# A state-space layer whose row split moves to GpSimd, whose load block is merged, and whose result is added to x by TensorE

## The reference, cut to what matters

```python
xn = layernorm(layernorm(x)) * gamma + beta
u, z = split(xn @ in_w.T)              # 256 features each
u = silu(causal_conv(u, 4 taps) + conv_b)
x_dbl = u @ xproj_w.T                  # 8 dt ranks, 16 B rows, 16 C rows
dt = softplus(x_dbl[:8] @ dt_w.T + dt_b)
for t in time:                         # 16 states for each feature
    h = exp(dt * A) * h + dt * B * u
    y = sum_n(h * C)
y = (y + u * D) * silu(z)
out = y @ out_w.T
# result: x + layernorm(x) + out_fwd + out_bwd
```

## Time and profile before

| | us |
|---|---|
| median of three runs | 2711.14 (2708.47 to 2712.14) |
| the profiled execution | 2711.35 |
| its span, first to last instruction | 2709.6 |
| first `step` of the layer | 69.28 |
| last x added in the layer | 1030.76 |
| VectorE busy in the span | 2064.6 (76%) |
| TensorE busy in the span | 2362.9 (87%) |
| GpSimd busy in the span | 1190.6 (44%) |

### The profile page before, as it was taken

The page is one execution under the profiler, slowest core; times in us unless marked ns, Lnnn a source line. Parts: engine busy times, 40 slices in busy tenths (PEclk is TensorE's granted clock), DMA queues, the critical chain, the costliest instruction groups (busy, mean ns, idle before and its releaser), DMA issues. The chain is left out here.

```text
span 2709.6 us, 45904 instructions
## 1 busy us (share of the span) xinstructions
PE 2362.9 (87%) x14688; PEld 1562.3 (58%) x14688; DVE 2064.6 (76%) x2993; ACT 1378.1 (51%) x2475; POOL 1190.6 (44%) x868
## 2 busy tenths in 40 slices
PE   2788888878888877997799996999999989978997
PEld 1333333333333325775688885666666667757776
DVE  2999999999999995776455554888888867755555
ACT  3666676666666643664322222666666656632100
POOL 4677777777777773333100002455555433330000
PEclk9899999999999997998799997999999989978999
DMA  3222222222222222000000000000000010000000
GB/s 104 65 72 71 75 70 67 71 70 74 70 72 74 71 66 64 12 12 25 0 1 1 0 1 6 1 0 0 0 0 0 1 52 12 12 2 5 8 8 12
DMA packets 72794, 89.88 MB, mean 33 GB/s; under 512 B 27062, under 2 KB 38368, under 8 KB 72176
## 3 DMA queue, kind: packets, MB, share of 16 engines
q1 hardware_dynamic: 72176, 88.13, 11.2%
q10 hardware_dynamic: 512, 0.53, 0.1%
HBM read 86.00 MB, written 2.62 MB: 33 GB/s over the span
## 5 line engine op out<-in xcount | busy, mean ns | idle before, releaser
L822 POOL TENSOR_TENSOR m_hc<-m_h,m_cs 128x1024 f32<-128x1024 f32 x256 | 602.6, 2358 | 247.3 <-DVE m_h L742 246.7
L742 DVE TENSOR_TENSOR_SCAN m_h<-m_da,m_pdb 128x1024 f32<-128x1024 f32 x256 | 585.1, 2286 | 25.1 <-DVE m_pdb L708 3.7
L475 PE MATMUL m_py<-m_hc,ident 128*128 128x512 f32 x1024 | 508.5, 621 | 1.9 <-POOL m_hc L822 1.9
L645 ACT ACTIVATE m_da<-m_dt,m_aneg 128x508 f32<-128x508 f32 x512 | 333.5, 709 | 138.8 <-DVE m_h L742 108.0
L475 PEld LDWEIGHTS m_py<-m_hc,ident 128*128 128x128 f32 x1024 | 200.4, 198 | 222.6 <-issue 208.0
L708 DVE TENSOR_TENSOR m_pdb<-m_du,m_pdb 128x1024 f32<-128x1024 f32 x256 | 308.8, 1206 | 11.4 <-POOL m_du L798 11.4
L462 PE MATMUL m_pdb<-m_bcrow,m_sel 96*128 96x512 bf16 x256 | 100.7, 394 | 161.2 <-DVE m_h L742 159.4
L1797 POOL TENSOR_TENSOR d_pr<-d_pr,d_rden 128x512 f32<-128x512 f32 x128 | 133.1, 1040 | 177.2 <-DVE d_rden L1728 177.2
L1429 ACT ACTIVATE c_act_of<-c_pg 128x512 f32<-128x512 f32 x144 | 86.1, 598 | 237.1 <-PE c_pg L213 231.7
L1075 ACT ACTIVATE x_prT<-x_pt 77x512 f32<-77x512 f32 x256 | 137.8, 586 | 134.2 <-PE x_pt L977 133.3
L462 PEld LDWEIGHTS m_pdb<-m_bcrow,m_sel 96*128 96x128 bf16 x256 | 25.5, 100 | 296.1 <-DVE m_h L742 250.6
(11 more groups left out here) (261 smaller groups left out, 5264.7 us busy)
## 6 DMA issues: line engine op xcount, KB each, us to landing
m_cs<-crow SPq DMA_DIRECT2D x256, 256.0 KB, 3.1
cw_gu<-in_C_gu SPq DMA_DIRECT2D x1, 2304.0 KB
x<-in_x SPq DMA_DIRECT2D x8, 256.0 KB, 5.0
fw_w<-in_F_w SPq DMA_DIRECT2D x1, 2048.0 KB
out_x<-x SPq DMA_DIRECT2D x8, 256.0 KB, 2.3
bm_mrow<-in_B_mrow SPq DMA_DIRECT2D x1, 1232.0 KB, 6.3
x_ctxT<-in_B_ctxT SPq DMA_DIRECT2D x32, 38.5 KB, 1.8
x_mask<-in_B_mrow SPq DMA_DIRECT2D x32, 38.5 KB, 2.8
```

The lines of the kernel that those rows point to most:

```text
L475: ins = mm(py[:, c, :], S.ident[:, :], hc[n % BUF][:, c, :], start=False, stop=n == NS - 1)
L645: A_(dst, src, ACT.Exp, scale=aneg[:, d, c, n:n + 1]).then_inc(s["da_ready"], 1)
L742: V.tensor_tensor_scan(h[n % BUF][:, way], da[n % BUF][:, d:d + CH * GT][:, way], pdb[:, b:b + 2, :].rearrange("p c t -> p (c t)")[:, way] ...
L822: P.tensor_tensor(hc[n % BUF][:, :, :], h[n % BUF][:, :].rearrange("p (c t) -> p c t", c=CH), bc(cs[n % BUF][:, :], 1, CH), ALU.mult).then ...
```

## The change

Three things change in the first layer.

1. **Row split on GpSimd.** ScalarE's copy to frow takes rows 0 to 119 of pm[1], not 96 to 119. GpSimd takes rest = frow - bcrow in slot 9 and writes block 2 of rest minus bcrow straight into bcrow in slot 11. VectorE's L695 and L699 and ScalarE's copy L615 are gone. GpSimd does its parts only after hc of the slot before. TensorE's second dt product waits for row_hi in place of row_rest, and row_ready now comes from GpSimd.
2. **Merged load block.** `load_layer` and its barrier are gone. SP issues x of group 0, the identity, and the weights in three sets, then x of the seven other groups, the masks and the next layer's weights. The layernorm's scalars go to VectorE (`moments`, with bn_aggr), except for the two powers, which stay on GpSimd. The set-up on VectorE has a new order: group 0's statistics and scalars, taps of direction 0, sel, aneg, taps of direction 1, skip, ident_bf, the statistics and scalars of the other 28 sequences, the mask rows.
3. **Result added by TensorE.** `project_out` begins each of its four blocks with an identity product that brings x into pm[0], and ScalarE copies pm[0] to x (`store_x`) in slot 10, behind the two row copies. VectorE's L716 is gone. The statistics move from slot 9 to slot 12.

```diff
@@ project_out (TensorE, slot 8) @@
+                    pe.wait_ge(s["xres_ready"], g + 1)
                     for i in range(GS):
+                        mm(pm[0][:, i * D:(i + 1) * D], S.ident[:, :], S.x[:, bass.ds(g * GS + i, 1), :],
+                           start=True, stop=False)
                         for c in range(CH):
                             ins = mm(pm[0][:, i * D:(i + 1) * D], ys[:, c, i * T:(i + 1) * T],
-                                     W.outw[:, d, c, :], start=c == 0, stop=c == CH - 1)
+                                     W.outw[:, d, c, :], start=False, stop=c == CH - 1)
@@ scan (ScalarE) @@
+                        add = n == 10 and not (isinstance(u, int) and u == 0)
+                        if add:
+                            act.wait_ge(s["o_mm"], u)
                         if nxt:
                             nxt(n)
+                        if add:
+                            store_x(u - 1, g if d else g - 1)
@@ front (GpSimd) @@
+                    if at in (None, 9):
+                        pool.wait_ge(s["row_hi"], u + 1)
+                        if due(2 * u):
+                            pool.wait_ge(s["row_mid"], 2 * u)
+                        if at is None:
+                            pool.wait_ge(s["r2_ready"], 2)
+                        else:
+                            pool.wait_ge(s["hc_ready"], NS * (u - 1) + at)
+                        P.tensor_tensor(rest[0:96, :], frow[d][0:96, :], bcrow[d][0:96, :],
+                                        ALU.subtract).then_inc(s["row_rest"], 1)
+                        pool.wait_ge(s["row_rest"], u + 1)
+                    if at in (None, 11):
+                        pool.wait_ge(s["row_mid"], 2 * u + 2)
+                        if at is not None:
+                            pool.wait_ge(s["hc_ready"], NS * (u - 1) + at)
+                        P.tensor_tensor(bcrow[d][64:96, :], rest[64:96, :], bcrow[d][64:96, :],
+                                        ALU.subtract).then_inc(s["row_ready"], 1)
+                        pool.wait_ge(s["row_ready"], u + 1)
@@ SP @@
+                load_x(0)
+                sp.dma_start(S.ident[:, :], ident_d).then_inc(s["ident_in"], 16)
+                W.first.load(sp)
+                W.then.load(sp)
+                W.load(sp)
+                for g in range(1, NG):
+                    load_x(g)
+                masks.load(sp)
+                ahead.load(sp)
@@ set-up (VectorE) @@
+                dve.wait_ge(x_in[0], 16)
+                S.next_stats(dve, 0, s["stats"])
+                dve.wait_ge(s["stats"], 1)
+                moments(0, LN_PARTS[0])
+                dve.wait_ge(W.first.loaded, W.first.all())
+                taps(0)
...
+                for g in range(1, NG):
+                    dve.wait_ge(x_in[g], 16)
+                    S.next_stats(dve, g, s["stats"])
+                dve.wait_ge(s["stats"], NG)
+                moments(1, LN_PARTS[1])
                 find_batches_with_keys(nc, dve, masks)
```

More of the change, by code:

```diff
@@ L167, in all @@
         return 16 * len(self.parts)
[L169 to L196, removed]
 def walk_groups(eng, body):
@@ L341, in mamba_layer @@
         s = {n: A.sem(n) for n in names}
+        x_in = [A.sem(f"x_in{g}") for g in range(NG)]
         crow_out = [A.sem(f"crow_out{d}") for d in range(2)]
@@ L427, in front @@
                     if at in (None, 7):
+                        if at is None:
+                            pe.wait_ge(W.then.loaded, W.then.all())
                         pe.wait_ge(s["us_ready"], CH * (u + 1))
@@ L626, in front, with store_x @@
                             rescale(g + 1)
+                def store_x(u, g):
+                    A_(seqs(S.x, g), pm[0][:, :].rearrange("p (i t) -> p i t", t=T), ACT.Copy
+                       ).then_inc(s["x_ready"], 1)
                 def gate_in(u, d):
@@ L664, in scan @@
                         sum_up(u, d)
+                        act.wait_ge(s["o_mm"], u + 1)
+                        store_x(u, g)
                 drive(act, front, scan, par)
@@ L670, in _, with moments @@
                 V = nc.vector
+                def moments(part, cols):
+                    n = part + 1
+                    lo, hi = cols.start, cols.stop
+                    for b in range(lo, hi):
+                        ins = V.bn_aggr(mv[:, b, :], S.bn[:, b, :])
+                    ins.then_inc(s["aggr"], 1)
+                    dve.wait_ge(s["aggr"], n)
+                    mean, var, r1 = mv[:, cols, 0], mv[:, cols, 1], S.rstd[:, cols]
+                    V.tensor_scalar(ve[:, cols], var, LN_EPS, None, ALU.add).then_inc(s["ve_ready"], 1)
+                    dve.wait_ge(s["r1_ready"], n)
+                    V.tensor_tensor(r1sq[:, cols], r1, r1, ALU.mult).then_inc(s["sq_ready"], 1)
+                    dve.wait_ge(s["sq_ready"], n)
+                    V.tensor_tensor(v2[:, cols], var, r1sq[:, cols], ALU.mult).then_inc(s["v2_ready"], 1)
+                    dve.wait_ge(s["v2_ready"], n)
+                    V.tensor_scalar(ve2[:, cols], v2[:, cols], LN_EPS, None, ALU.add).then_inc(s["ve2_ready"], 1)
+                    V.tensor_scalar(r1p[:, cols], r1, 1.0, None, ALU.add)
+                    V.scalar_tensor_tensor(mr1[:, cols], mean, -1.0, r1, ALU.mult, ALU.mult)
+                    dve.wait_ge(s["r2_ready"], n)
+                    V.tensor_tensor(r12[:, cols], r1, r2[:, cols], ALU.mult).then_inc(s["r12_ready"], 1)
+                    dve.wait_ge(s["r12_ready"], n)
+                    V.scalar_tensor_tensor(mr12[:, cols], mean, -1.0, r12[:, cols], ALU.mult, ALU.mult
+                                           ).then_inc(s["ln_ready"], 1)
@@ new lines, in taps @@
+                def taps(d):
+                    V.tensor_tensor(wtap[:, d], W.convw[:, d], bc(W.win_u[:, d], 1, TAPS), ALU.mult
+                                    ).then_inc(s["wtap_ready"], 1)
+                dve.wait_ge(x_in[0], 16)
[4 more added lines that the diff above has]
+                taps(0)
+                dve.wait_ge(W.then.loaded, W.then.all())
@@ L672, in _ @@
+                V.tensor_copy(sel[:, :, :], bc(W.sel32[:, :], 2, 128)).then_inc(s["sel_ready"], 1)
+                dve.wait_ge(s["aexp_ready"], 1)
+                V.tensor_scalar(aneg[:, :, :, :], aexp[:, :, :, :], -1.0, None, ALU.mult).then_inc(s["aneg_ready"], 1)
                 dve.wait_ge(W.loaded, W.all())
-                for d in range(2):
-                    ins = V.tensor_tensor(wtap[:, d], W.convw[:, d], bc(W.win_u[:, d], 1, TAPS), ALU.mult)
-                ins.then_inc(s["prep"], 1)
@@ L676, in _ @@
-                V.tensor_copy(sel[:, :, :], bc(W.sel32[:, :], 2, 128)).then_inc(s["prep"], 1)
+                taps(1)
+                dve.wait_ge(s["ident_in"], 16)
                 for d in range(2):
```

149 lines of the change are left out of this document (64 added, 85 removed).

## The result

The changed kernel takes 2669.97 us (median, 2664.09 to 2673.01) against 2711.64 (2708.47 to 2712.87) for the kernel before: a ratio of 0.9845, 95% interval 0.9824 to 0.9867. That is 41.7 us faster, where 29.8 were forecast. The profiled execution took 2664.09, its span is 2662.3.

The account below looks back on a forecast made before the run. VectorE was taken to pace the changed layer's scans. Start -17.2, unit 0 -2.2, fourteen units -11.9, last unit -0.4 and end +1.9 sum to -29.8, from 2711.35 to 2681.5 us; own range 2673 to 2691, full range 2656 to 2700.

Parts of the forecast that it names:

- the scans: From the first `step` to the last scan's start: forecast 14.5 us shorter, 11.9 of it in fourteen units.
- the start: Before the first `step`: GpSimd's queue sets when rest runs; first `step` at 52.0, 17.2 us saved.
- the cost of the end: Last unit's projection: 24 records on TensorE instead of 16, costing 1.9 us more.
- The chain in front of it: GpSimd's subtraction (1.27), two row copies and `store_x` (0.63 each) delay TensorE's dt products to A+8.3, A being scan 8's start.
- the wait in slot 11: VectorE waits 2 us in every unit for TensorE's `spread` 12, taken to end 6.34 behind the dt products' start.
- The statistics: In seven units the statistics now stand in front of scan 12 on VectorE and take 1.05 us.
- Unit 0: First unit, with no result to wait for: gains the two subtractions in full, 2.2 us.
- the last unit: Last unit of the changed layer: loses only VectorE's L716, a gain of 0.4 us.
- Costs nothing: Slot 8 on TensorE: four identity products, 0.9 us, end before the wait for x_ready and so cost nothing.
- The clock holds: Rival: TensorE's clock holds or its queue isn't late, so VectorE doesn't wait; 36.4 us gained in fourteen units, 2657; chance 0.22.
- The moved work eats itself up: Rival: GpSimd's subtraction takes 2.38 or TensorE's stretches are longest; units lose 0.2 to 0.3, about 2698; chance 0.13.
- Slower: Rival: TensorE's low clock lasts through slot 12, losing 3.3 us a unit, 46 in all, 2739; chance 0.04.

Follow-up runs that it names:

- e1: The changed kernel with `store_x` moved ahead of the decay and the row copies on ScalarE in slot 10; 2652.5 us, ratio 0.9773.
- e2: The changed kernel with dt products reading all 120 rows of frow, the added weight rows being zeros; 2653.09 us, ratio 0.9790.
- u1: The changed kernel with the row split back on VectorE and ScalarE, merged load block and addition by TensorE kept; 2691.59 us, ratio 0.9925.
- e4: The changed kernel with the second power of the seven other groups moved behind unit 0's row split in GpSimd's queue; 2661.43 us, ratio 0.9818.
- u3: The changed kernel with the addition to x and the statistics back on VectorE in slot 9; 2669.03 us, ratio 0.9845.
- x_rest_twice: The changed kernel with GpSimd taking the first subtraction twice in every unit; 2701.44 us, ratio 0.9959.
- u2_old_start: The kernel before with the row split on GpSimd and the addition by TensorE, keeping the old load block, barrier and set-up; 2684.0 us, ratio 0.9896.

## Why the prediction was right, and which terms were mis-sized

The direction, the mechanism and each place named in the sum were right. The time, 2669.97, lies in the range of 2656 to 2700, and 3 us below the forecast's own 2673 to 2691. Two gains were forecast too small, the scans by 10.3 and the start by 2.5, and the cost of the end by 0.7.

- **VectorE set the pace, and was then held by TensorE in slot 11: shown.** Waits that end with `spread` came in 12 of 14 units, and e1 and e2 take them away from two sides, with 18 us less stretch each. Undoing part 1 (u1) brings back 14.7 us of stretch with the two subtractions.
- **The chain in front of it was as costed.** GpSimd's subtraction took 1.15 (taken: 1.27, from L1356). The dt products started at A+8.16 to 8.35 (8.3), with 1.46 to 1.72 of idle time in front (1.6), released by `store_x` of 0.60 (0.63).
- **The term that was off most is the wait in slot 11: "I take the same 6.34".** TensorE's stretch measured 5.72. The waits were then 17.6 us in 12 units, 1.26 over all fourteen, not 2.0 in every one. That is 10.4 us less than forecast, as much as the 10.3 by which the scans beat the sum. Of it 8.7 is 0.62 times fourteen, and most of the rest is that the dt products started at A+8.20 on average and not at 8.3. The mean of before was taken over values of 5.1 to 7.5 whose spread I had not explained, and with the idle time in front of the `spread` before the products, not in front of the products. After, the same products behind nearly the same gap took from 4.08 to 7.11, so a mean over fourteen can well move by some tenths. Whether the 0.62 is this scatter or the new place of the gap isn't shown, nor why the clock falls in one unit and not in its neighbour.
- **The statistics were mis-sized the other way round.** I left them at 1.05 in front of scan 12. In e1, where nothing waits in these units, scans 8 to 12 span 14.0 without them and 14.6 with them, so they cost 0.6: the four records run as one piece of 0.86 that starts before the `step` in front has ended. Over seven units that is 3.2 us. Against these 13.6 stand 1.1 us more between scan 12 and the next scan 8, 0.7 by which scans 8 to 12 of before span less in fourteen units than I had (242.4, not 243.2), and some 1.5 of other short waits.
- **Unit 0 gained 2.2 (16.20 to 14.00) and the last unit 0.4 (14.41 to 14.00), as forecast.**
- **The start was set by GpSimd's queue, as said: shown by e4.** The second power ended at 34.79 and not at 37.3, and the first `step` came 2.5 earlier than forecast. The cast of sel took 1.22 and not the 3.31 that I took from before, but that gave nothing: VectorE idled 3.33 behind it for ScalarE's exp (L562), and a cast of 3.31 would have ended at 13.1 and been hidden there as well. What came early is that exp: VectorE went on at 14.30, and not at about 16.2, as I had estimated. That is 1.9 of the 2.5, and the 28 statistics, 5.7 and not 6.0, are most of the rest. The distance from rest to the first `step` was 14.6 (forecast 14.7).
- **The end cost 2.6, not 1.9.** TensorE's 24 records took 5.5 where the 16 took 3.78: 1.7 more, so the term of 1.9 was about right. The other 0.9 lies behind the last statistics: from their end to the layer's end it is 1.78 before (1032.36 to 1034.14) and 2.70 after (989.42 to 992.12). It isn't `store_x`, for u3, which has none, has 2.71 there. What it is stays open. With part 3 undone the distance from the last scan to the layer's end is 18.0, with it 20.1.
- **"Costs nothing" for the identity products held,** but part 3 as a whole bought nothing in the scans once part 1 was in. The sum took 0.67 a unit off VectorE and gave it back as a wait without saying so; u3 shows it.

On the rivals. *The clock holds* came true in two units of fourteen, and in e2 as a whole: its estimate of 36.4 in fourteen units compares with 40.2 in e2 (42.8, less 2.2 for unit 0 and 0.4 for the last), and most of the difference is that of the statistics (7 times 0.45). *The moved work eats itself up* fell with 1.15. The Trainium skill's warning (Perfetto Trace Analysis, "Optimizing Scalar/DVE Operations") that offloading between VectorE and GpSimd might not help did not come true here: the scans took 2286 ns and `step` 1206 to 1207 before and after, and u1 puts the moved subtractions at 14.7 us of stretch. The prediction gave the reason: what is left on VectorE has one input in PSUM. That this is why the warning did not bite was not tried by a run of its own. *Slower* did not come; x_rest_twice shows what would have led there, since a step of 2.3 us in its place already ate all the gain of the scans (953.8 against 947.3).

## What to carry to other kernels

- When an engine's work is taken away, ask at once which engine's queue it will next wait for, and cost that queue up to the instruction that it needs. Here a copy of 0.6 us, behind two others on ScalarE, held TensorE, whose clock then fell, and moving that copy forward gave 18 us without any work less.
- A mean over repeats with a wide spread (5.1 to 7.5 for the same work) is a sign of a state that isn't understood. A term taken from it can move when its surroundings change, here from 6.34 to 5.72, and the range should carry that, times the number of repeats.
- Gains of parts that hide in the same wait don't add: undo each alone, and in pairs, before keeping a part that lengthens the end.

## What the runs showed of the hardware

- **The depth of the products mattered for the granted clock.** With TensorE idle for 1.36 to 1.72 in front, the dt products of 8 rows were followed by a granted clock of 0.50 in 12 units of 14, those of 120 rows in none. They have the same columns, and at full clock both take 1.95 us (e1, e2). Zero weights were enough: the 112 added rows of the weights are zeros, though the rows of frow that they meet are not. The 8 rows are rows 96 to 103, and whether their place matters beside their number was not tried.
- **The idle time mattered too.** Behind 2.67 to 2.94 of it the clock fell in 6 of 14 units even with 120 rows. With 8 rows and at most 0.2 of it in front (e1, and ten units of u1) the clock fell in 5 units of 24. In u3, where the dt products follow `spread` 11 at once but TensorE idles 1.0 to 2.4 in front of that `spread`, it fell in 11 of 14.
- **A delay in front of such products cost more than itself:** 1.2 us more in the chain made 2.2 us a unit, since the time to the end of `spread` 12 grew by 1.0 as well.
- **A cast to bf16 of 96x2048 took 1.22 us alone and 3.31 while GpSimd cleared da** (3.62 from 24.15 before; 1.81 to 5.43 after, when the cast came at 9.75). It took 3.31 again in u2_old_start, and both times it ended 1.1 behind the clearing. So these two engines can hold each other up with no semaphore between them. The Trainium skill (SBUF — State Buffer, "Who interferes with whom") says that a VectorE copy or cast in a mode that uses both port pairs and a GpSimd instruction block each other for the whole instruction; the durations agree, but no row shows in which mode the cast ran.
- **A GpSimd subtraction of 96x512 with one bf16 operand took 1.15 us, and one of 32x512 the same 1.15:** a third of the rows saved nothing. VectorE needed 1.82 for the latter next to GpSimd's hc, and 0.68 in unit 0 (57.18 before), where GpSimd ran nothing; this bears out the prediction's reading of L699.
